# Two-layer conditioned transformer block: layer 1's modulation loads and products moved to later slots, with the first MLP's weights of layer 0 moved four slots later

## The chip, the cores and the metric

The kernel runs on one core of one Trainium2 chip. The metric is the device time of one execution in microseconds. Five engines work in parallel, each through its own instruction list in order: PE (matrix products), DVE (vector), ACT (scalar functions; it also issues some DMAs), POOL and SP (which here only issues DMAs). They wait for each other and for DMAs through semaphores.

## The reference

The input is x, 32 samples of 256 tokens by 288 channels, and one condition vector of 288 channels a sample. Two layers follow each other, and both have this form:

```
mod = silu(cond) @ w_mod + b_mod            # 6 x 288 values a sample: shift, scale, gate for each half
h = layernorm(x) * (1 + scale_a) + shift_a
q, k, v = split(h @ w_qkv + b_qkv)          # 16 heads of 18 channels
q, k = layernorm(q) * g_q, layernorm(k) * g_k   # layer 0 only
x = x + gate_a * (softmax(q k^T / sqrt(18)) v @ w_proj + b_proj)
h = layernorm(x) * (1 + scale_m) + shift_m
x = x + gate_m * (gelu(h @ w1 + b1) @ w2 + b2)  # hidden width 1152
```

All of it is float32. Matrix products are made from operands split in a high and a low part ("hi", "lo"), which are multiplied in three terms.

## The kernel before

The work is a software pipeline over 64 sample passes: passes g = 0 to 31 are layer 0, passes 32 to 63 are layer 1. Time is divided into slots T, from -66 on, and a new pass begins every 16 slots (`SPAN = 16`). Each engine has one function (`slots_pe`, `slots_act`, `slots_dve`, `slots_pool`, `slots_sp`) that runs over all slots and, in each, issues what is due. A slot is not a time: it only sets the order of an engine's list, and semaphore waits do the rest. An engine that waits for nothing runs ahead of the others. The numbers by which things are due are constants at the head of the file, and pass g is due at slot 16g plus the constant. A bank of the matrix unit's output memory is given to each use by `bank_table`, which walks over the same slots.

Around the change these steps matter:

- **Stacks.** The scores of pass g need q and k spread over partitions in a "stack". SP copies them there with 18 DMAs: six small ones of 32 KB (`place_tails`, L1303) and twelve of 128 KB (L1352). For pass 1 they are due at slots -1 to 2, for pass 2 at 15 to 18, for pass 3 at 31 to 34. PE's first score product of pass g (L862, waiting for all 18 DMAs) is due at slot 16g - 12: slot 4 for pass 1, 20 for pass 2, 36 for pass 3, 52 for pass 4.
- **Norm of q and k (layer 0).** ACT writes the reciprocal root (L1031) just after that same slot, SP stores it to device memory (L1324, slot 16g - 26) and reads it back spread out (L1327, L1328, slot 16g - 25, which waits until the store has landed). DVE multiplies with it (L1131, slots 16g - 20 to 16g - 17), ACT and POOL split the result (L1024, L1292), and SP stacks it.
- **Modulation of layer 1.** SP loads two biases and six weight blocks of 324 KB (`load_mod`, L434) at the slots of `MOD_LOAD`. PE makes six products (L565, `MOD_AT[4:]`), and DVE adds the bias to each (L575, `MOD_ROW_AT[4:]`); the first of each waits for all eight loads, since they share a semaphore. DVE copies the rest channels (L583, `MOD_REST_AT[1]`), PE turns the rows (`MOD_TR[1]`), and SP stores them (L1380, 252 KB, `MOD_STORE[1]`).
- **Weights of layer 0's MLP.** They lie over the space of the preparation, so `load_w1` on ACT's queue (1584 KB and a bias in 5 DMAs, `W_AT[0]`) waits for the modulation of layer 1 to be turned and stored; `load_w2` (1296 KB, `W2_AT[0]`) is behind it. The split in hi and lo is on ACT (L752 and L753 for w1, L766 for w2) at `W1_SPLIT[0]` and `W2_SPLIT[0]`, and on DVE (L757, L759, L762 for w1, L770 for w2) one slot later. The first MLP product is due at slot 49.
- **Staging of layer 1's attention weights.** SP loads a third of them at slots 6, 14 and 22, ACT and DVE split it at 16/17, 24/25 and 32/33, and SP stores it (1152 KB for the first two) at 20, 28 and 36.

In one slot SP takes its work in this order: copies of o, the placing of the negated maxima (L1318), the store and the read-back of the roots, the stacks, loads of x, the gate, the store of x, and then this code, which the change touches:

```
if T == MOD_LOAD[0]:   # waits for mod_mm 6, mod_rows_ready 1, scores 1, then the two biases
for j, at in enumerate(MOD_LOAD):
    if T == at: load_mod(q, 1, slice(C * j, C * j + C), S["w_mod_loaded", 2])
if T in MOD_STORE: ...
if T == 18: q.wait_ge(S["mod_stored", 0], 16); q.wait_ge(S["mod_stored", 1], 16)
```

Of the kernel before, what the change touches and what calls it, by code (L numbers as in the profile page):

```python
# [11 lines left out]
B, N, C = 32, 256, 288  # L12
# [53 lines left out]
SPAN = 16  # L66
# [23 lines left out]


MOD_OUT_AT, QKV_HI_AT, QKV_LO_AT, PROJ_REST_AT, PROJ_SCALE_AT, PROJ_HI_AT, PROJ_LO_AT = -56, (-57, -50), (-54, -49), -30, -16, -15, -14
MOD_AT, MOD_ROW_AT = (-36, -36, -27, -26, 6, 7, 8, 9, 10, 11), (-28, -28, -26, -25, 6, 7, 8, 9, 10, 11)
MOD_REST_AT, MOD_TR, MOD_STORE, MOD_LOAD = (-25, 11), (-19, 13), (-13, 15), (-11, -9, -7, -3, -1, 1)
W_AT, W1_SPLIT, W2_SPLIT = (20, SPAN * (B - 1) + 51), (32, SPAN * (B - 1) + 58), (36, SPAN * (B - 1) + 64)
W2_AT = (21, SPAN * (B - 1) + 59)
STAGE_AT = [16, 24, 32]
NEW_QK_AT, NEW_V_AT, NEW_PROJ_AT = SPAN * (B - 1) - 24, SPAN * (B - 1) - 20, SPAN * (B - 1) + 32

# [117 lines left out]
def build(nc, a, out):  # L217
    outer = ExitStack()
    with outer:
# [511 lines left out]
        def load_w1(q, l):  # L731
            if l == 0:
                q.wait_ge(S["proj_w_lo"], 2)
                q.wait_ge(S["spots_ready"], 5)
                q.wait_ge(S["mod_turned"], 24)
                q.wait_ge(S["mod_rows_ready"], 2)
                q.wait_ge(S["mod_stored", 0], 16)
                q.wait_ge(S["mod_stored", 1], 16)
            else:
                q.wait_ge(S["fc1"], FC1_USES * B)  # L740
            w, bias, _ = MLP_NAMES[l]
            for dst, src in raw_moves(w1_raw[:, 2:5, :], w, bias, slice(0, MLP)):
                q.dma_start(dst, src).then_inc(S["w1_loaded"], 16)

        def load_w2(q, l):
            if l > 0:
                q.wait_ge(S["fc2"], TT * B)
            q.dma_start(w2_raw[:, 1], a[MLP_NAMES[l][2]].rearrange("(c p) n -> p c n", p=P)).then_inc(S["w2_loaded"], 16)
# [209 lines left out]
        def slots_act(q):  # L958
            for T in SLOTS:
# [102 lines left out]
                for l in range(LAYERS):  # L1062
                    if T == W_AT[l]:
                        load_w1(q, l)
                    if T == W2_AT[l]:
                        load_w2(q, l)
# [231 lines left out]
        def slots_sp(q):  # L1298
# [7 lines left out]
            for T in SLOTS:  # L1306
# [70 lines left out]
                if T in MOD_STORE:  # L1377
                    l = MOD_STORE.index(T)
                    q.wait_ge(S["mod_rows_ready"], l + 1)
                    q.dma_start(mod_d[l], rows[l][:]).then_inc(S["mod_stored", l], 16)  # L1380
                if T == 18:
                    q.wait_ge(S["mod_stored", 0], 16)
                    q.wait_ge(S["mod_stored", 1], 16)
                if T + 10 in STAGE_AT:
# [44 lines left out]
        @block.sync  # L1429
        def _(q):  # L1430
            prep_sp(q)
            slots_sp(q)
# [25 lines left out]
```

## Time and profile before

| | us |
|---|---|
| median of 3 runs | 2560.09 (2556.29 to 2560.41) |
| the profiled execution | 2560.63 |
| its span | 2558.8 |

The span is what the trace covers; the profiled execution lasted 1.8 us longer than it. Busy shares of the span: PE 93%, PE weight loads 78%, DVE 72%, ACT 64%, POOL 28%. In the page's 40 slices of 64 us PE is busy 5, 5, 6 and 8 tenths in the first four and 9 tenths in nearly all others.

### The profile page before, as it was taken

The numbers are of one execution on the slowest core, as the hardware profiler recorded it, in microseconds if no ns is written. First come the engines' busy times: TensorE is split into PE (matmuls) and PEld (weight loads), VectorE is DVE, ScalarE is ACT, GpSimd is POOL, SyncE is SP. The second block draws the span as 40 slices with busy tenths as digits, with TensorE's granted clock in tenths as the row PEclk, the third lists the DMA queues.
The fourth block names the chain that finished last, engine by engine and source line by source line (L and its number), as shares of the span: only waits on it lengthen the run. The fifth ranks groups of instructions, "written<-read, shape, count | busy, mean of one in ns | idle before, by whom it ended". The sixth has DMA issues, their size and how long they took to land.

```text
span 2558.8 us, 56620 instructions
## 1 busy us (share of the span) xinstructions
PE 2368.6 (93%) x21219; PEld 1988.2 (78%) x21219; DVE 1842.1 (72%) x3456; ACT 1626.4 (64%) x3049; POOL 708.4 (28%) x938
## 2 busy tenths in 40 slices
PE   5568999999999999999899899999999999999998
PEld 3346878878888887887787788888888888888878
DVE  6357777777777777777677777777777777777764
ACT  3256666676676666666566666666676666666653
POOL 2012332332332333233222122222222222223212
PEclk8778999999999999999999999999999999999989
DMA  3776757757656666666856755565566655565531
GB/s 99 134 172 107 122 114 117 122 114 122 116 114 117 116 118 116 114 119 113 141 89 114 144 98 101 95 112 106 97 103 102 114 95 101 97 113 102 95 65 42
DMA packets 259208, 280.91 MB, mean 110 GB/s; under 512 B 25930, under 2 KB 243212, under 8 KB 258936
## 3 DMA queue, kind: packets, MB, share of 16 engines
q1 hardware_dynamic: 245840, 250.24, 56.4%
q10 hardware_dynamic: 13096, 27.04, 4.1%
q8 instruction: 170, 2.79, 0.5%
q14 instruction: 102, 0.84, 0.2%
HBM read 101.86 MB, written 26.73 MB: 50 GB/s over the span
## 4 chain that ended last, share of the span: by engine, by line
PE 50%; DVE 14%; DMA 12%; SPq 7%; issue 7%; POOL 5%; ACT 4%; DVEq 0%; POOLq 0%; ACTq 0%
PE psum L783 11%; DMA attn_k_stack<-attn_qk_hi 9%; PE psum L873 7%; SPq L1352 6%; PE psum_exp L783 5%; PE psum_max L783 5%; DVE attn_maxima L1093 5%; PE psum_exp L849 4%; PE psum L933 4%; PE psum L934 4%; PE psum L935 4%; PE psum_max L862 3%; DVE attn_qk_centred L1131 3%; POOL attn_qk_lo L1292 2%; PE psum L790 2%
## 5 line engine op out<-in xcount | busy, mean ns | idle before, releaser
L969 ACT ACTIVATE attn_probs<-psum_exp 128x1024 f32<-128x1024 f32 x512 | 527.0, 1029 | 401.1 <-PE psum_exp L849 388.2
L1093 DVE TENSOR_REDUCE attn_maxima<-psum_max 128x4 f32<-128x1024 f32 x512 | 620.4, 1212 | 90.1 <-PE psum_max L862 86.1
L1266 POOL TENSOR_TENSOR mlp_x<-mlp_x,mlp_gated 128x288 f32<-128x288 f32 x128 | 103.1, 805 | 1051.6 <-DVE mlp_gated L1110 1051.6
L783 PE MATMUL psum<-attn_ln_split,w_qkv_split 128*128 128x256 f32 (+3 forms) x2240 | 337.6, 296 | 10.1 <-DVE attn_ln_split L1200 6.8
L933 PE MATMUL psum<-mlp_w_fc_hi,mlp_hidden_hi 128*128 128x288 f32 x1152 | 341.7, 297 | 2.9 <-DVE mlp_w_fc_lo L770 2.0
L934 PE MATMUL psum<-mlp_w_fc_lo,mlp_hidden_hi 128*128 128x288 f32 x1152 | 341.4, 296 | 0.0
L935 PE MATMUL psum<-mlp_w_fc_hi,mlp_hidden_lo 128*128 128x288 f32 x1152 | 341.0, 296 | 0.0
L783 PEld LDWEIGHTS psum<-attn_ln_split,w_qkv_split 128*128 128x128 f32 (+3 forms) x2240 | 282.7, 182 | 59.1 <-issue 25.5
L862 PE MATMUL psum_max<-attn_k_stack,attn_q_stack 62*128 62x256 f32 x2048 | 218.9, 292 | 91.5 <-DMA attn_k_stack<-attn_qk_hi 62.7
L873 PE MATMUL psum<-attn_probs,attn_v 128*32 128x256 f32 x4096 | 282.7, 395 | 1.1 <-ACT attn_probs L969 1.1
L849 PE MATMUL psum_exp<-attn_q_stack,attn_k_stack 64*128 64x256 f32 x2048 | 260.2, 332 | 24.2 <-DMA attn_q_stack<-attn_neg_max_lo 12.0
L1224 DVE CAST mlp_hidden_hi<-mlp_hidden 128x512 fp32r<-128x512 f32 (+1 forms) x320 | 127.4, 398 | 175.0 <-ACT mlp_hidden L1051 175.0
L862 PEld LDWEIGHTS psum_max<-attn_k_stack,attn_q_stack 62*128 62x128 f32 x2048 | 159.4, 189 | 113.2 <-DMA attn_k_stack<-attn_qk_hi 56.6
L849 PEld LDWEIGHTS psum_exp<-attn_q_stack,attn_k_stack 64*128 64x128 f32 x2048 | 155.1, 186 | 116.7 <-issue 65.0
L1110 DVE TENSOR_TENSOR mlp_gated<-psum,mlp_gate_and_gated_bias 128x288 f32<-128x288 f32 x128 | 58.3, 456 | 247.3 <-PE psum L935 247.1
L783 PE MATMUL psum_exp<-mlp_ln_split,mlp_w_fc_stacked 128*128 128x256 f32 (+1 forms) x1792 | 229.0, 285 | 2.2 <-ACT attn_probs L969 2.2
L783 PE MATMUL psum_max<-mlp_ln_split,mlp_w_fc_stacked 128*128 128x256 f32 (+1 forms) x1792 | 225.4, 283 | 0.0
L783 PEld LDWEIGHTS psum_exp<-mlp_ln_split,mlp_w_fc_stacked 128*128 128x128 f32 (+1 forms) x1792 | 220.1, 192 | 3.7 <-issue 3.7
L933 PEld LDWEIGHTS psum<-mlp_w_fc_hi,mlp_hidden_hi 128*128 128x128 f32 x1152 | 218.5, 190 | 3.7 <-DVE mlp_w_fc_lo L770 2.3
L783 PEld LDWEIGHTS psum_max<-mlp_ln_split,mlp_w_fc_stacked 128*128 128x128 f32 (+1 forms) x1792 | 219.5, 192 | 0.0
L934 PEld LDWEIGHTS psum<-mlp_w_fc_lo,mlp_hidden_hi 128*128 128x128 f32 x1152 | 218.4, 190 | 0.0
L935 PEld LDWEIGHTS psum<-mlp_w_fc_hi,mlp_hidden_lo 128*128 128x128 f32 x1152 | 218.3, 190 | 0.0
(170 smaller groups left out, 4203.8 us busy)
## 6 DMA issues: line engine op xcount, KB each, us to landing
attn_q_stack<-attn_qk_hi SPq DMA_DIRECT2D x256, 128.0 KB
attn_k_stack<-attn_qk_hi SPq DMA_DIRECT2D x256, 128.0 KB
attn_o_and_sums<-attn_o_transposed SPq DMA_DIRECT2D x256, 128.0 KB, 5.0
mlp_gate_and_gated_bias<-modulation ACTq DMA_DIRECT2D x64, 288.0 KB, 4.1
attn_qk_squares<-qk_rstd SPq DMA_DIRECT2D x32, 512.0 KB
attn_q_stack<-attn_qk_lo SPq DMA_DIRECT2D x128, 128.0 KB
attn_k_stack<-attn_qk_lo SPq DMA_DIRECT2D x128, 128.0 KB
attn_x<-in_x_dram SPq DMA_DIRECT2D x32, 288.0 KB, 8.0
```

What stands on the lines that cost most here:

```text
L783: mm = q.matmul(to, lhs, rhs, start=(i == 0), stop=(i == 6))
L849: mm = q.matmul(ps_exp[:, h, t * N:t * N + N], k_st[i][r, p, t * P:t * P + P], q_st[q_place(g)][r, p, :], start=True, stop=True)
L862: mm = q.matmul(ps_max[:, h, t * N:t * N + N], q_st[q_place(g)][r, p, t * P:t * P + P], k_st[i][r, p, :], start=True, stop=True)
L873: mm = q.matmul(bank[32 * i:32 * i + VW, 0:N], v_sb[g % V_RING][:, t, grp * PV_HEADS + i, :, :].rearrange("p r c -> p (r c)"), probs[pair ...
L933: q.matmul(bank[:, 0:C], h_hi[:, c, cols], w2_hi[:, c, :], start=(c == 0), stop=False)
L934: q.matmul(bank[:, 0:C], h_hi[:, c, cols], w2_lo[:, c, :], start=False, stop=False)
L935: mm = q.matmul(bank[:, 0:C], h_lo[:, c, cols], w2_hi[:, c, :], start=False, stop=(c == CHUNKS - 1))
L969: q.activation(probs[r][:], ps_exp[:], ACT.Exp, scale=SCORE_SCALE).then_inc(S["exps"], 1)
L1093: q.tensor_reduce(maxes[g % 2][:, p // QUARTER, :, p % QUARTER, :], ps_max[:].rearrange("p a (t n) -> p a t n", t=TT), AX.X, ALU.max).then ...
L1224: q.tensor_copy(hi, hidden[use % 2][:, 0:n, :]).then_inc(S["h_hi"], 1)
L1266: q.tensor_tensor(xt, xt, gated2[:], ALU.add).then_inc(S["added2"], 1)
L1352: q.dma_start(fp(st[r:r + MAIN_D, :, :]), fp(parts[order[j]][:, c, :])).then_inc(S["stack_loaded", i], 16)
```

## The change

Only constants change, and the slot of one wait:

```diff
-MOD_AT, MOD_ROW_AT = (-36, -36, -27, -26, 6, 7, 8, 9, 10, 11), (-28, -28, -26, -25, 6, 7, 8, 9, 10, 11)
-MOD_REST_AT, MOD_TR, MOD_STORE, MOD_LOAD = (-25, 11), (-19, 13), (-13, 15), (-11, -9, -7, -3, -1, 1)
-W_AT, W1_SPLIT, W2_SPLIT = (20, SPAN * (B - 1) + 51), (32, SPAN * (B - 1) + 58), (36, SPAN * (B - 1) + 64)
-W2_AT = (21, SPAN * (B - 1) + 59)
+MOD_AT, MOD_ROW_AT = (-36, -36, -27, -26, 10, 11, 12, 13, 14, 15), (-28, -28, -26, -25, 10, 11, 12, 13, 14, 15)
+MOD_REST_AT, MOD_TR, MOD_STORE, MOD_LOAD = (-25, 15), (-19, 17), (-13, 19), (3, 4, 5, 6, 7, 8)
+MOD_DONE = 22
+W_AT, W1_SPLIT, W2_SPLIT = (24, SPAN * (B - 1) + 51), (36, SPAN * (B - 1) + 58), (40, SPAN * (B - 1) + 64)
+W2_AT = (26, SPAN * (B - 1) + 59)
...
-                if T == 18:
+                if T == MOD_DONE:
                     q.wait_ge(S["mod_stored", 0], 16)
                     q.wait_ge(S["mod_stored", 1], 16)
```

The loads of layer 1's modulation go from slots -11 to 1 to slots 3 to 8, its products from 6 to 11 to 10 to 15, its turn from 13 to 17 and its store from 15 to 19. The load of w1 goes from slot 20 to 24 and that of w2 from 21 to 26; the splits go from 32 and 36 to 36 and 40 (ACT), with DVE's part one slot behind. The entries for layer 1 (the second of each pair) are as before.

## Rows read from the trace of the kernel before

**Rows 1.** The page, part 1: busy time of each engine over the span.
```profile
PE 2368.6 (93%) x21219; PEld 1988.2 (78%) x21219; DVE 1842.1 (72%) x3456; ACT 1626.4 (64%) x3049; POOL 708.4 (28%) x938
```

**Rows 2.** Busy time by window: length, engines, PEclk, DMA share, GB/s.
```profile
75.30:111.90 36.60, 18.12 (x117) 13.98 (x117) 16.09 (x27) 11.83 (x28) 4.65 (x7) 0.69 0.77 141
111.90:162.60 50.70, 31.73 (x249) 18.96 (x249) 22.13 (x45) 19.76 (x42) 5.08 (x7) 0.80 0.64 133
162.60:205.70 43.10, 28.91 (x216) 20.03 (x217) 32.59 (x57) 28.60 (x56) 7.92 (x11) 0.78 0.81 183
205.70:247.70 42.00, 37.41 (x313) 29.21 (x313) 30.98 (x53) 25.58 (x52) 9.70 (x13) 0.87 0.60 109
247.70:285.60 37.90, 36.46 (x338) 30.76 (x338) 28.71 (x53) 26.19 (x53) 12.29 (x17) 1.00 0.68 115
```

**Rows 3.** PE's waits from 60 to 252 us: total, times, longest.
```profile
PE psum_max L862 <- DMA attn_k_stack<-attn_qk_hi: 45.2, 5, 17.4
```

**Rows 4.** The chain of waits from 60 to 300 us: start, length, what.
```profile
79.02 3.69 DMA qk_rstd<-attn_qk_rstd
...
83.35 5.56 DMA attn_qk_squares<-qk_rstd
...
103.39 8.48 DMA attn_k_stack<-attn_qk_hi
...
149.10 13.47 DMA attn_k_stack<-attn_qk_hi
...
168.01 7.39 DMA qk_rstd<-attn_qk_rstd
...
197.78 7.87 DMA attn_k_stack<-attn_qk_hi
```

**Rows 5.** Busy time by window, two stretches of 4 us.
```profile
84.00:88.00 4.00, 0.71 (x5) 0.39 (x5) 2.04 (x4) 0.00 (x0) 0.00 (x0) 0.82 0.84 205
...
112.00:116.00 4.00, 4.00 (x36) 1.98 (x37) 1.77 (x3) 0.38 (x1) 0.00 (x0) 0.50 0.00 1
```

**Rows 6.** SP's instructions in order of time: start, length, what.
```profile
94.80 0.44 SPq L434 DMA_DIRECT2D prep_w_mod<-in_L_cond_W_ada_dram  x1
...
121.43 0.55 SPq L1327 DMA_DIRECT2D attn_qk_squares<-qk_rstd  x1
...
140.84 0.44 SPq L1380 DMA_DIRECT2D modulation<-prep_mod_rows  x1
141.33 1.29 SPq L1352 DMA_DIRECT2D attn_q_stack<-attn_qk_hi  x2
```

**Rows 7.** ACT's queue, first DMA of w1.
```profile
144.63 0.42 ACTq L743 DMA_DIRECT2D mlp_w_fc_raw<-in_L_cond_w_dram  x1
```

**Rows 8.** DMA issues from 83.9 to 85.2 us: KB each, us to landing.
```profile
prep_w_mod<-in_L_cond_W_ada_dram SPq DMA_DIRECT2D x2, 324.0 KB, 6.5
```

**Rows 9.** PE's instructions in order of time, 112 to 163 us.
```profile
116.05 2.23 PE L565 MATMUL psum<-prep_w_mod,prep_silu_transposed 96*32 96x288 f32 x6
...
125.96 3.10 PE L565 MATMUL psum<-prep_w_mod,prep_silu_transposed 96*32 96x288 f32 x12
...
162.62 0.80 PE L862 MATMUL psum_max<-attn_k_stack,attn_q_stack 62*128 62x256 f32 x4 [17.38 <-DMA attn_k_stack<-attn_qk_hi]
```

**Rows 10.** DVE's instructions in order of time, 131 to 211 us.
```profile
131.81 0.72 DVE L583 COPY prep_mod_rows_rest<-prep_mod_rows 32x96 f32<-32x96 f32 x4
...
195.38 2.57 DVE L757 TENSOR_TENSOR mlp_w_fc_stacked<-mlp_w_fc_raw,mlp_w_fc_stacked 128x2304 fp32r<-128x2304 f32 x1
197.85 1.43 DVE L759 SCALAR_TENSOR_TENSOR mlp_w_fc_stacked<-mlp_ln_split,s_one_on_low_weight_rows,mlp_w_fc_raw 98x1152 fp32r<-98x1152 f32 x1
...
207.68 2.85 DVE L770 TENSOR_TENSOR mlp_w_fc_lo<-mlp_w_fc_raw,mlp_w_fc_hi 128x2592 fp32r<-128x2592 f32 x1
```

**Rows 11.** Busy time by window, the stretch behind slot 36.
```profile
206.50:222.70 16.20, 12.22 (x106) 7.81 (x108) 15.68 (x25) 9.03 (x19) 2.66 (x4) 0.82 0.45 98
222.70:247.70 25.00, 24.39 (x205) 20.82 (x203) 15.30 (x29) 16.55 (x33) 7.04 (x10) 0.92 0.69 107
```

## The prediction, made before the changed kernel was run

> **What bounds the kernel now.** I began with the busy shares: PE is busy 93% of the span [rows 1], so over the whole it is the bound, and only a stretch in which it stands still can give much. The change touches nothing behind slot 41, and slots run to 1079, so I cut the start into stretches between the first score products of passes 0, 1, 2, 3, 4 and 5 (slots -12, 4, 20, 36, 52, 68) [rows 2]. A pass takes 37.9 us in the last of them, where PE is busy 36.46 us of it. The four before take 36.6, 50.7, 43.1 and 42.0, with PE busy 18.1, 31.7, 28.9 and 37.4. PE's waits name the cause: 45.2 us in five waits for a stack, the longest 17.4 [rows 3]. The chain of waits shows the last DMA of each stack landing 8.48 us after its issue for pass 1, 13.47 for pass 2 and 7.87 for pass 3 [rows 4]. So the start is bound by a loop: root stored, read back, norm, split, 18 stack DMAs, landing, first score product, next root. A gain counts only if a stack lands earlier, a loss counts if it delays the next loop, and whatever is won or lost by slot 52 stays to the end, since nothing behind it waits for a clock. I work out how each of the four first score products moves; + is earlier.
>
> **Slot 4 (111.9 us now).** Three things leave this loop. (a) Two modulation loads are issued right behind the read-back of pass 1's roots, which takes 5.56 us on the chain [rows 4]. Between 84 and 88 us the DMAs move 205 GB/s [rows 5], and at that rate the read-back's 576 KB take 2.9 us, with some 1.2 us before the first data: 4.1 us. I take +1.5, bounds 0 and 2. (b) Two more loads stand among the stack's DMAs [rows 6] (the one shown is issued at 94.80). Each costs SP about 0.5 us of issue, 1.0 together, and 324 KB at 205 GB/s, 1.6 us, 3.2 together. If issue binds the gain is 1.0, if the DMA engines bind it is 3.2; I take +2.0. (c) The loads are now issued behind the stack, three of them before it has landed. If they share the engines with its tail they cost up to 1.5 us; I take -0.5. Sum +3.0, bounds +0.5 and +5.
>
> Here a rule can be weighed. Of the read-back's 5.56 us [rows 4] some 4.4 carry data, which at the rate above is 0.9 MB, and the read-back has 0.59: bytes of later DMAs of the same queue pass before it has landed. The Trainium skill ("DMA: Bandwidth & Descriptors", section on queues, rings and completion order) says that on each DMA engine descriptors of one queue are consumed in ring order. By that rule alone loads behind cost nothing to what is ahead: (a) would be 0, (c) would be 0, and the slot would gain 2.0 in place of 3.0. The trace leans against its plain reading, and the sum goes by the trace.
>
> **Slot 20 (162.6 us now, 50.7 behind slot 4).** Gains first. w1 starts on ACT's queue at 144.63 [rows 7] while pass 2's stack is being issued (from 141.33) [rows 6]. It is the difference that I see between this stack's 13.47 us and the 7.87 and 8.48 of its neighbours: 5.0 to 5.6 us [rows 4]. At slot 24 w1 is issued after PE's slot 20, so it is out of the way: +5.0. The modulation store (0.44 us of issue, ahead of the big copies) goes behind them: +0.5.
>
> Then the new wait. In the loop SP reads the roots back at slot 7, 9.5 us behind PE's slot 4 (121.43) [rows 6]. The blocks of slots 7 and 8 are issued behind the two read-backs, the last at about 9.5 + 1.7 = 11.2 us. Two blocks behind a read-back landed 6.5 us after issue [rows 8]. So the last lands 17.7 us behind slot 4; 14.8 if nothing stands before it (an estimate: 6.5 less the read-back's 2.9), 19.7 if it takes as long as a stack's last DMA, 8.48 [rows 4]. PE gets to its first modulation product (slot 10) earlier than now: that product begins at about 127.5 (the second half of the row of 12), 15.6 behind slot 4, less four products that move back (2.23 and three of some 1.6, 6.9 with their overlap) [rows 9] = 8.7 us. The products and the scores behind them then stand still for 9 us, and slot 10 is 17.7 - 15.6 = 2.1 us later than now. DVE waits with PE for the same loads, and the norm of pass 2 (slots 12 to 15) is queued behind on both. After a standstill the granted clock is 0.50 (the 1.2 GHz level) [rows 5]; I price its return at 1.5 us, bounds 0 and 2.5, by the first product's 2.23 us against 1.6. The copies of slot 11 (0.72 us and a product) [rows 10] leave the front of slot 12's negated maxima: +1.1. Net -2.5, bounds +1 and -5.5. Products in slots 12 to 15 are 6.5 us on PE, beside a stack whose 12 us of issue they mostly hide under; o's last copy at slot 18 may come late: -0.5. Without that cover they would cost up to 3.
>
> Sum for the stretch: +5.0 + 0.5 - 2.5 - 0.5 = +2.5, bounds -3.5 and +6.
>
> **Slot 36 (205.7 us now).** w2 no longer runs beside the store of pass 3's roots, which lands after 7.39 us, against 3.69 for pass 1 [rows 4]: +3.7. But w1 and w2, 2.9 MB, now fall between ACT's slot 24 and the stack, together with a read-back, x and 1.15 MB of stage stores. The DMA share of this stretch is already 0.81 [rows 2]; w1's 1.6 MB more are 8.8 us at the stretch's 183 GB/s and 7.9 at 205, and the share leaves 43.1 x 0.19 = 8.2. So the stack may be issued sooner and land no sooner. ACT's five issues (some 2 us) delay an exponential that PE reaches late anyway. The split of w1 leaves slots 32 and 33, but that shortens only PE's way to a wait for the stack. I take 0, bounds +3 and -5.
>
> **Slot 52 (247.7 us now).** DVE is busy 15.68 of the 16.2 us behind slot 36's scores, and PE 24.39 of the 25 after that [rows 11]: no room on either. In DVE's full stretch now stands w2's low part, 2.85 us. It will hold w1's 2.57 + 1.43 + 0.27 = 4.27 us at slot 37 and w2's 2.85 at slot 41, both ahead of pass 4's norm at slot 44 [rows 10]: 4.3 us more, of which I see nothing that is hidden. ACT's part of w1 falls in PE's wait. I take -4.3, bounds -1.4 (only slot 37's excess counts) and -6.5 (with ACT's 2.4 us of w2 at slot 40).
>
> **Sum.** +3.0 + 2.5 + 0 - 4.3 = +1.2 us. The profiled execution took 2560.63 (span 2558.8 and 1.8 around it), which gives 2559.4. It lies 0.5 above the median of the runs, so against the median I say 2559.
>
> **Rivals.**
> - *The stacks' gain stands, and the rest is hidden (faster).* The last block lands with its 3.6 us or the clock costs nothing (slot 20 gains 5.5 rather than 2.5), the earlier store of the roots gives 2 us at slot 36, and half of DVE's 4.3 us falls into waits for PE. +3 + 5.5 + 2 - 2.2 = +8.3: 2552. For it speaks the 13.47 us, a large and plain stall; against it the full DVE.
> - *The DMA engines in the third stretch (slower).* w1 and w2 pile up before pass 3's stack. If 8.8 us of transfers meet only some 3 us of free share in the part from the load to the stack, the stack lands about 5 us later, and DVE's 4.3 is added in full: +3 + 2.5 - 5 - 4.3 = -3.8, 2564. With the clock's cost at its bound it is 2566. It decides as soon as the stage stores are still in flight when the big copies are issued. Share 0.81 speaks for it; that the stretch held w2 already speaks against it.
> - *It doesn't do what it says:* loads issued behind the stack are served beside it, and pass 1's stack lands as late as now: +0.5 at slot 4, 2561.5.
>
> **How the numbers follow.** Forecast 0.50, hidden rest 0.28, DMA pile 0.15, no earlier stack 0.07. What a measurement of this kernel tells from no change is 0.2%, 5.1 us: below 2555.0 or above 2565.2. The forecast's own spread is some 4 us either way, which leaves 0.08 of all cases at the fast end and 0.05 at the slow one; with most of the first rival (0.22) faster is 0.30, with under half of the second and some of the third slower is 0.14, and the same has 0.56. The range, 2551 to 2566, reaches over both rivals' times.
>
> **What would show it.** Right: PE's wait at slot 4 begins at the same place and ends about 3 us sooner; a new wait of PE for w_mod at slot 10, near 9 us; pass 2's last stack DMA landing within 7 to 9 us; the stretch to slot 36 near 43 us with DMA share above 0.9; the stretch to slot 52 near 46 us with w1's split inside. Wrong: no wait at slot 10, which would leave PE's early start to the norm of pass 2 and give 3 us or more; a stretch of 42 us to slot 52; or a stack 3 that lands after 12 us.

## The result, and the profile after

The changed kernel takes 2571.77 us (median of 5 runs, 2567.29 to 2572.78); the kernel before, timed with it, 2556.29. The ratio is 1.0055, 95% interval 1.0042 to 1.0067. By the medians it is 15.5 us slower (11 to 17 by the interval), where 2559 and no change were forecast, and outside the range of 2551 to 2566. The profiled execution took 2572.48 us, 11.85 more than that of the kernel before.

I cut its start as before, between the first score products of passes 0 to 5. This is the view of busy time by window: length, then PE, PE's weight loads, DVE, ACT, POOL, PEclk, DMA share, GB/s. Lines of the changed kernel are one higher than before (L863 is the score product, L566 the modulation product).

```profile
76.60:110.50 33.90, 17.03 (x117) 13.07 (x117) 16.08 (x27) 11.55 (x28) 4.62 (x7) 0.75 0.57 84
110.50:166.60 56.10, 38.79 (x251) 22.07 (x251) 22.76 (x45) 19.85 (x42) 4.50 (x7) 0.71 0.63 127
166.60:215.00 48.40, 27.07 (x217) 19.11 (x217) 26.66 (x54) 26.23 (x55) 8.17 (x11) 0.75 0.88 207
215.00:261.70 46.70, 38.52 (x313) 30.15 (x313) 35.26 (x56) 27.73 (x53) 9.66 (x13) 0.83 0.50 93
261.70:299.80 38.10, 36.53 (x340) 30.82 (x340) 28.71 (x53) 26.16 (x53) 12.28 (x17) 1.00 0.68 114
```

Against [rows 2] the four stretches changed by -2.7, +5.4, +5.3 and +4.7 us, together +12.7; the fifth is as it was (38.1 against 37.9). Another 1.3 us of the trace's difference lies ahead of slot -12, where the change has moved nothing; that slot comes between 74.4 and 76.6 us in the twelve traces of this case. The forecast had -3.0, -2.5, 0 and +4.3. So the first and the last came out as numbers, and the two in the middle did not.

PE's waits in the changed kernel, from 75 to 262 us (total, times, longest), hold one that was not there:

```profile
PE psum_max L863 <- DMA attn_k_stack<-attn_qk_hi: 39.2, 5, 13.8
PE psum_max L863 <- DVE attn_maxima L1094: 10.7, 4, 6.0
PE psum L942 <- DVE attn_maxima L1094: 10.3, 4, 4.2
PE psum L566 <- DMA prep_w_mod<-in_L_cond_W_ada_dram: 9.4, 1, 9.4
```

PE's instructions in order of time show that wait and what follows it. Each row of x6 is one product:

```profile
129.19 3.06 PE L566 MATMUL psum<-prep_w_mod,prep_silu_transposed 96*32 96x288 f32 x6 [9.39 <-DMA prep_w_mod<-in_L_cond_W_ada_dram]
...
133.33 3.08 PE L566 MATMUL psum<-prep_w_mod,prep_silu_transposed 96*32 96x288 f32 x6
...
136.66 3.09 PE L566 MATMUL psum<-prep_w_mod,prep_silu_transposed 96*32 96x288 f32 x6
...
147.19 1.64 PE L566 MATMUL psum<-prep_w_mod,prep_silu_transposed 96*32 96x288 f32 x6
```

The standstill of 9.4 us is the one forecast. The products then take 3.1 us and not 1.6: the granted clock of the stretch behind it is 0.50, the 1.2 GHz level, although PE is busy all the time (the clock comes back at 142.5, 13.3 us after the first product began):

```profile
129.20:142.00 12.80, 12.80 (x47) 5.16 (x51) 4.49 (x8) 2.25 (x3) 0.00 (x0) 0.50 0.01 2
```

In the third stretch the chain of waits goes through x for the residual, which SP asks for behind the read-back and POOL needs first, 16.28 us after its issue; the roots' store lands in 4.03, where it took 7.39 [rows 4]:

```profile
171.49 4.03 DMA qk_rstd<-attn_qk_rstd
175.53 0.57 SPq L1328
...
176.15 0.57 SPq L1329
...
176.77 16.28 DMA mlp_x<-in_x_dram
193.05 0.07 issue
193.12 0.93 POOL mlp_x L1263
```

DVE's longest wait there is for the read-back, which lands 15.2 us after its second issue (176.15 to 191.37):

```profile
DVE attn_qk_centred L1132 <- DMA attn_qk_squares<-qk_rstd: 9.3, 1, 9.3
```

w2, issued at 175.70 on ACT's queue, ran beside it and took 22.8 us. From 175.5 to 177.3 us the packets of ACT's queue (q10) take 68% of the 16 DMA engines' time and those of SP's (q1) 29%:

```profile
mlp_w_fc_raw<-in_L_cond_w_dram ACTq DMA_DIRECT2D x1, 1296.0 KB, 22.8
...
q10 hardware_dynamic: 80, 0.37, 68.1%
q1 hardware_dynamic: 66, 0.13, 29.2%
```

In the fourth stretch the chain holds the splits of both weights on DVE, where before it held w2's alone [rows 10]:

```profile
217.04 2.46 DVE mlp_w_fc_stacked L758
219.50 1.33 DVE mlp_w_fc_stacked L760
...
231.13 2.85 DVE mlp_w_fc_lo L771
```

### The profile page after: what moved, and what is told of

Its sections match the earlier page's. It is cut to its first block, busy times and chain, and to the rows that moved or that the text cites. A ratio compares the mean times of both kernels' runs of the same rounds, so it can differ in the third digit from the quotient of the medians.

```text
span 2570.7 us, 56620 instructions
## 1 busy us (share of the span) xinstructions
PE 2372.7 (92%) x21219; PEld 1990.3 (77%) x21219; DVE 1839.4 (72%) x3456; ACT 1624.5 (63%) x3049; POOL 705.4 (27%) x938
## 4 chain that ended last, share of the span: by engine, by line
PE 51%; DVE 14%; DMA 12%; SPq 8%; issue 7%; POOL 5%; ACT 4%; DVEq 0%; POOLq 0%; ACTq 0%
PE psum L784 12%; DMA attn_k_stack<-attn_qk_hi 9%; PE psum L874 7%; SPq L1353 6%; PE psum_exp L784 5%; PE psum_max L784 5%; DVE attn_maxima L1094 5%; PE psum_exp L850 4%; PE psum L934 4%; PE psum L935 4%; PE psum L936 4%; PE psum_max L863 3%; DVE attn_qk_centred L1132 2%; PE psum L791 1%; POOL attn_qk_lo L1293 1%
## 5 line engine op out<-in xcount | busy, mean ns | idle before, releaser
L1094 DVE TENSOR_REDUCE attn_maxima<-psum_max 128x4 f32<-128x1024 f32 x512 | 620.6, 1212 | 85.2 <-PE psum_max L863 81.3
L863 PE MATMUL psum_max<-attn_k_stack,attn_q_stack 62*128 62x256 f32 x2048 | 219.3, 293 | 84.8 <-DMA attn_k_stack<-attn_qk_hi 55.9
L863 PEld LDWEIGHTS psum_max<-attn_k_stack,attn_q_stack 62*128 62x128 f32 x2048 | 160.4, 190 | 105.5 <-DMA attn_k_stack<-attn_qk_hi 48.3
```

Source lines behind the costliest of these rows:

```text
L863: mm = q.matmul(ps_max[:, h, t * N:t * N + N], q_st[q_place(g)][r, p, t * P:t * P + P], k_st[i][r, p, :], start=True, stop=True)
L1094: q.tensor_reduce(maxes[g % 2][:, p // QUARTER, :, p % QUARTER, :], ps_max[:].rearrange("p a (t n) -> p a t n", t=TT), AX.X, ALU.max).then ...
```

## The experiments

Ten kernels, all timed against the kernel before. The table gives each one's four stretches (us between first score products, from the start times of PE's rows) and the ratio with its interval. In the first, third and fourth stretch, kernels that share the order of work agree within 0.4 to 1.3 us. The second is less sure: four kernels do the same up to slot 20 (changed, modulation only, splits back, weights later) and take 56.1, 56.5, 56.9 and 53.3 us. Each kernel has one trace. The total times do not follow the stretches closely: "weights later" is 7.7 us above the kernel before by its stretches and 14.2 by the medians, "dense after the wait" 13.9 and 23.9. The trace of the kernel before is itself one of its slower executions (2560.63 us, where the medians of its runs beside the other kernels are 2555.1 to 2559.3).

| kernel | to slot 4 | to 20 | to 36 | to 52 | sum | ratio (95%) |
|---|---|---|---|---|---|---|
| before | 36.6 | 50.7 | 43.1 | 42.0 | 172.3 | 1 |
| changed | 33.9 | 56.1 | 48.4 | 46.7 | 185.1 | 1.0055 (1.0042 to 1.0067) |
| weights only | 36.6 | 45.8 | 49.1 | 46.1 | 177.6 | 1.0022 (1.0011 to 1.0032) |
| modulation only | 33.5 | 56.5 | 45.4 | 41.6 | 177.0 | 1.0023 (1.0012 to 1.0033) |
| splits back | 33.6 | 56.9 | 48.1 | 41.8 | 180.3 | 1.0037 (1.0023 to 1.0051) |
| weights later | 33.5 | 53.3 | 47.2 | 46.0 | 180.0 | 1.0058 (1.0042 to 1.0075) |
| loads early | 33.6 | 41.9 | 48.4 | 46.6 | 170.4 | 1.0002 (0.9992 to 1.0011) |
| warm | 33.6 | 49.5 | 49.4 | 46.4 | 178.8 | 1.0027 (1.0014 to 1.0040) |
| dense after the wait | 33.6 | 57.7 | 48.9 | 46.1 | 186.2 | 1.0082 (1.0063 to 1.0101) |
| early, old weight slots | 33.7 | 44.1 | 46.0 | 41.5 | 165.3 | 0.9965 (0.9952 to 0.9977) |
| early, w2 at 37 | 33.7 | 43.2 | 41.7 | 46.8 | 165.5 | 0.9975 (0.9961 to 0.9989) |
| early, w2 at 42 | 33.6 | 43.9 | 41.4 | 43.4 | 162.2 | 0.9966 (0.9953 to 0.9979) |

**Weights only.** The kernel before with the weights' line of the change:

```diff
-W_AT, W1_SPLIT, W2_SPLIT = (20, ...), (32, ...), (36, ...)    # W2_AT 21
+W_AT, W1_SPLIT, W2_SPLIT = (24, ...), (36, ...), (40, ...)    # W2_AT 26
```

> The kernel before with only the MLP weights of layer 0 moved (w1 loaded at slot 24, w2 at 26, splits at 36 and 40), the modulation as before. Stretches between first score products: 36.6, 50.7, 43.1, 42.0 us before and 33.9, 56.1, 48.4, 46.7 after. My theory: the weights own one gain and two losses. Stretch to slot 4 stays 36.6; stretch to slot 20 falls to 45 to 46, since w1 no longer runs beside pass 2's stack; stretch to slot 36 is 47 to 49, since w1 and w2 now run beside pass 3's read-back (DVE's wait for attn_qk_squares near 9 us, 2 to 4 before); stretch to slot 52 is 46 to 47. Total 3 to 5 us slower than before. Rival: the two late losses come down from the standstill at slot 10 (low clock, late work), and then stretches three and four stay at 43 and 42 here, and the kernel is 5 us faster than before.

As my theory had it in all four stretches: -4.9 us in the second, +6.0 in the third (49.1, at the upper end) and +4.1 in the fourth, in a kernel that never stands still at slot 10. In its third stretch DVE waits 7.9 us for the read-back and x takes 15.58, as in the changed kernel. The rival is out: the two late losses belong to the weights. In time it is 5.6 us slower than before, a little more than the 3 to 5 expected.

**Splits back.** `W1_SPLIT[0]` 36 to 32 and `W2_SPLIT[0]` 40 to 36 in the changed kernel.

> The changed kernel with only the splits of the MLP weights back at slots 32 and 36. My theory: DVE's full stretch behind slot 36 holds 4.3 us less, so the stretch to slot 52 falls from 46.7 to 42 to 43 us and the others stay (33.9, 56.1, 48.4; w2's landing, 22.8 us after issue, is by then past). Some 4 us faster than the changed kernel, 8 to 10 slower than before. Rival: the fourth stretch is long because of the late stack or the low clock, and stays at 46 to 47.

The fourth stretch fell to 41.8 and nothing else moved by more than 0.8. DVE's busy time in it is again what it was before, 30.98 us [rows 2], against 35.26 in the changed kernel:

```profile
214.80:256.60 41.80, 37.28 (x311) 29.18 (x311) 30.98 (x53) 25.57 (x52) 9.75 (x13) 0.88 0.57 104
```

**Weights later.** `W_AT[0]` 24 to 28 and `W2_AT[0]` 26 to 32 in the changed kernel.

> The changed kernel with w1 loaded at slot 28 and w2 at 32 (24 and 26), splits unchanged. My theory: pass 3's read-back then has the DMA engines to itself: DVE's wait for it falls from 9.3 us to under 3, and the stretch to slot 36 from 48.4 to 42 to 45 us (the loads may now lie beside the stack, which costs up to 3). Other stretches as in the changed kernel, unless w1's later landing holds ACT at slot 36. 4 to 6 us faster than the changed kernel. Rival: the read-back is late for the stage stores, not for w1 and w2, and the third stretch stays at 48.

Half right. DVE's wait for the read-back in this stretch fell to 0.3 us, so w1 and w2 were what held it, but the stretch fell only to 47.2, and in time the kernel is no faster than the changed one (1.0058 against 1.0055). The same transfers, issued at 173.9 and 190.3, now stood in the way of the negated maxima and of pass 3's stack, as the chain of this kernel shows (a last stack DMA takes 6.8 to 8.7 us in stretches where no MLP weights run beside it):

```profile
179.00 12.00 DMA attn_q_stack<-attn_neg_max_lo
...
196.52 13.53 DMA attn_k_stack<-attn_qk_hi
```

The second stretch is 2.8 us shorter than the changed kernel's, although no part of the edit lies ahead of slot 20. PE does the same work in the same order there and stands still for 9.8 us. What differs is the clock: it comes back 6.5 us after the first product began (at 128.89), within the second product, and the third is already at full speed:

```profile
133.03 2.81 PE L566 MATMUL psum<-prep_w_mod,prep_silu_transposed 96*32 96x288 f32 x6
...
135.97 1.64 PE L566 MATMUL psum<-prep_w_mod,prep_silu_transposed 96*32 96x288 f32 x6
```

In the changed kernel, "splits back" and "modulation only" the same work had to go on for 13.3, 14.1 and 13.3 us first. Why it took half as long here no run shows.

**Loads early.** The six blocks are issued before SP waits for the roots of pass 2:

```diff
-MOD_LOAD = (3, 4, 5, 6, 7, 8)
+MOD_LOAD = (3, 3, 4, 4, 5, 5)
```

> The changed kernel with the six modulation blocks loaded at slots 3, 3, 4, 4, 5, 5 in place of 3 to 8, so that SP issues all of them ahead of its wait for pass 2's roots. My theory: the last block lands by 118 us, PE does not stand still at slot 10 (9.4 us in the changed kernel), the clock stays up, and the stretch to slot 20 falls from 56.1 to 43 to 47 us; the roots' store may land 2 us later. 9 to 12 us faster than the changed kernel. Rival 1: the wait moves to the negated maxima at slot 8, which are then behind 2 MB of loads, and the gain is under 4. Rival 2: the products themselves at slots 10 to 15, not the wait, hold pass 2's norm, and the stretch stays above 51.

The second stretch fell by 14.2 us to 41.9, the shortest of all. PE's wait for the blocks is gone, and the clock is 0.91 over the stretch. Of the first rival there is a sign, a wait of PE of 2.6 us for the negated maxima, but not its cost:

```profile
109.40:151.30 41.90, 32.41 (x251) 19.92 (x251) 23.05 (x45) 19.98 (x42) 4.63 (x7) 0.91 0.83 171
```

The three later kernels with the same slots for the modulation took 44.1, 43.2 and 43.9: they wait 1.8 to 2.8 us at the same place, and at or just behind that wait the clock falls to 0.50 once more for some 3.5 us, which it doesn't do here. Against "weights only" (45.8), where the six products stand at slots 6 to 11, these four are 1.7 to 3.9 us better. So moving loads and products together was a gain (which of the two gives it, no run separates), and what spoilt it was how late the data were asked for.

**Modulation only.** The changed kernel with the weights' slots of before.

> The changed kernel with the MLP weights' slots as before (w1 20, w2 21, splits 32 and 36): the modulation's part of the change alone. ACT's slot 20 now waits for the modulation's store of slot 19, so w1 leaves about when pass 2's stack has landed. My theory: stretches 33.6, 56 to 58 (standstill and low clock as in the changed kernel), 43 to 46 (w1 and w2 lie ahead of pass 3's read-back), 42. Some 4 us slower than before, 8 faster than the changed kernel. Rival: w1 and w2 cost the third stretch as much wherever they stand, 48.

As expected, 45.4 in the third stretch and 41.6 in the fourth. Against the kernel before, w1 and w2 cost 2.3 us more in the third stretch when they start right behind pass 2's stack (w1 at 166.6), and 6.0 more when they start at slots 24 and 26.

**Warm.** The changed kernel with work in place of the standstill:

```diff
+if n == 4:      # the first of layer 1's products, slot 10
+    for i in range(40):
+        q.matmul(bank[:, 0:P], ident[:], ident[:], start=True, stop=True)
 mod_product(q, 2 + n, bank)
```

> The changed kernel, with 40 idle products (identity by identity, 128 columns, float32, some 0.2 us each at 2.4 GHz, 8 to 9 us together) put in PE's list at slot 10 ahead of the product that waits for the modulation's loads; they write a bank that this product overwrites. PE no longer stands still, it works through the wait. My theory: the standstill lets the granted clock fall to 0.50 and the six products then take 3.1 in place of 1.6 us; kept at work, the clock stays at 1.0 and the stretch to slot 20 falls by 5 to 8 us from 56.1, though the wait for the loads is the same. Rival: the clock comes down from the products themselves, or has no part, and the stretch stays above 54.

The added block took 9.09 us, PE then waited only 0.4 for the loads, and the stretch fell by 6.5 us. The products behind it take 1.6 us:

```profile
117.95 9.09 PE L839 MATMUL psum<-identity 128*128 128x128 f32 x80
127.47 1.64 PE L567 MATMUL psum<-prep_w_mod,prep_silu_transposed 96*32 96x288 f32 x6 [0.42 <-DMA prep_w_mod<-in_L_cond_W_ada_dram]
```

The first modulation product still begins 18.6 us behind slot 4, as in the changed kernel (18.7), so the wait is the same and the 6.5 us are the clock's. Against "weights later" (53.3), where the clock came back sooner, it is 3.8, and against "splits back" (56.9) 7.4.

**Dense after the wait.** 20 such products ahead of the second modulation product.

> The changed kernel with 20 identity products (128 by 128 weights, 0.23 us each at 2.4 GHz, twice that at 1.2) ahead of the second modulation product: added work of 5 to 9 us behind the standstill, none in it. It asks why the clock, which in the kernel before is back at 1.0 some 6 us after a standstill, takes 13 us in the changed one. Theory: the modulation products (96 by 32 weights) do not raise it and dense ones do; the clock is back within the added block and the products behind it take 1.6 in place of 3.1 us, which pays back 4 to 6 of the added 5 to 9 us. The stretch to slot 20 is 56 to 60. Rival: the low clock lasts 13 us whatever PE does, all products still take 3.1 us until then, and the stretch is 62 to 65.

The clock came back within the added block, and the next modulation products are at full speed:

```profile
128.04 3.06 PE L567 MATMUL psum<-prep_w_mod,prep_silu_transposed 96*32 96x288 f32 x6 [9.77 <-DMA prep_w_mod<-in_L_cond_W_ada_dram]
...
132.19 5.81 PE L839 MATMUL psum<-identity 128*128 128x128 f32 x40
137.93 1.64 PE L567 MATMUL psum<-prep_w_mod,prep_silu_transposed 96*32 96x288 f32 x6
```

5.8 us of added work lengthened the stretch by 1.6 against the changed kernel. The rival, 13 us whatever PE does, is out. But the theory isn't shown either: the clock came back 6.4 us after the first product began, and in "weights later" it came back after 6.5 with the modulation products alone. With one trace of each, this run can't tell the kind of work from that spread.

**Early loads with the old weight slots.**

> The modulation moved as in the change but its six blocks loaded at slots 3, 3, 4, 4, 5, 5, and the MLP weights' slots as before. My theory: 33.6, 42, 43 to 46, 42 us: 6 to 10 us faster than before. Rival: w1, which now starts when pass 2's stack has landed, delays the roots' store and read-back of pass 3 as in the changed kernel, the third stretch is 48, and the gain over before is 3 to 4.

165.3 us of stretches against 172.3 and a ratio of 0.9965, 8.4 us by the medians: the first version faster than before. The second stretch (44.1) is 2 us above what I expected, for the clock as told under "loads early". The third (46.0) is at the upper end of it: the roots' store takes 9.83 us there, beside w1 and w2.

**w2 at slot 37**, split at 45 and 46.

> As the one with early loads and the old weight slots, but w2 is loaded at slot 37 and split at 45 (ACT) and 46 (DVE). Its 1296 KB then lie behind pass 3's stack, where the DMA share is near 0, and its 2.85 us on DVE leave the full stretch behind slot 36. My theory: 33.6, 42, 42 to 44, 39 to 41 us: 3 to 5 us faster than the kernel with the old weight slots, 10 to 13 faster than before. Rival: the loop's next read-back (pass 4) meets w2, and the fourth stretch is 42 or more.

The third stretch came out (41.7, where w2 no longer runs), the fourth went the rival's way: 46.8. So the kernel is no faster than the one with the old weight slots (2550.5 and 2550.9 us). w2 was issued at 198.03, just ahead of the roots' store at 198.47, whose read-back could only be issued at 205.80, and its split stood in ACT's list ahead of the exponential of slot 45.

**w2 at slot 42**, split at 47 and 48, `MOD_DONE` 21 (ahead of the load of the gate in slot 22, which reads what it waits for).

> As the kernel with early loads, w1 at slot 20 and its split at 32, but w2 is loaded at slot 42, behind pass 4's read-back (slot 39) and not, as at slot 37, ahead of the roots' store, and split at 47 (ACT) and 48 (DVE), where DVE waits for the MLP. The wait for the modulation's store is at slot 21. Stretches of the kernel with w2 at slot 37: 33.7, 43.2, 41.7, 46.8 us. My theory: the first three stay and the fourth falls to 40 to 43, since the chain of the 46.8 held the roots' store at 7.3 us and ACT's split in the norm of pass 4. 12 to 16 us faster than before (0.9940 to 0.9955), 3 to 6 faster than the best so far. Rival: w2 collides with x and the negated maxima of slots 42 to 45 instead, and the fourth stretch stays at 46.

43.4 us in the fourth stretch and 162.2 in all, the least of any version. In time it is 2545.9 us in the median of 10 runs against 2555.1 for the kernel before; the ratio of 0.9966 is 8.7 us, less than the 12 to 16 expected, and within its interval the same as the version with the old weight slots. x for pass 1's residual, issued at 203.81 just before w2 at 203.86, takes 10.81 us in its chain (7.00 for pass 0), so w2 still collides with it.

## Why the prediction was wrong

**Slot 4, forecast +3.0: right as a number, in part by luck.** The gain is 2.7 us, and 2.9 to 3.1 in the other kernels with the modulation moved. Its terms came out otherwise. (a), the two loads behind the read-back, was to give 1.5: with nothing behind it the read-back takes 5.25 us here (4.8 to 5.0 in the others) against 5.56 [rows 4], so 0.3 to 0.8. (b), the two loads among the stack's DMAs, was to give 2.0: from the read-back's landing to the issue of the last stack DMA it is 1.4 us less. (c) was to cost 0.5: the last stack DMA took 7.95 us against 8.48, so loads issued behind the stack did not hold it. The store of the roots gives the last 0.35. By ring order alone (a) and (c) would have been 0 and the sum 2.0, and its terms are no further off than mine.

**Slot 20, forecast +2.5, measured -5.4: this is the step that failed most, by a term that was mis-sized.** The gain of w1's move was right (5.0 forecast, 4.9 in "weights only"). The wait was nearly right too: first product 17.7 us behind slot 4 forecast, 18.7 measured, a standstill of 9 forecast and 9.4 measured. What failed is "I price its return at 1.5 us, bounds 0 and 2.5, by the first product's 2.23 us against 1.6". "Warm" puts the term at 6.5 us in this kernel. The price was already too low for the kernel before: the product of 2.23 us [rows 9] is only the last work at the low clock there, and PE had then worked at 0.50 since slot 4, with score products of 0.80 us that later take 0.40. Its clock comes back 5.4, 5.9 and 3.7 us after the first score products at 111.9, 162.6 and 205.7, and at half speed each of these costs half its length, up to 3 us. The first modulation product of the changed kernel stands at the head of such a stretch and not at its end. That the stretch was then 13.3 us long was in no row of the kernel before, and why it was is open: with the same work it was 13.3, 14.1, 13.3 and 6.5 us in four kernels. Without the clock, "warm" still stands 3.7 us above "weights only", where my other terms made 1.0; 1.0 of the difference is the later landing of the blocks, and the rest, 1.7, I can't assign.

**Slot 36, forecast 0, bounds +3 and -5, measured -5.3: wrong, by a term put at nothing.** The rival of the DMA pile named the right cause and the right size, 5 us, and the wrong place. I looked for it at the stack. It came at the read-back (15.2 us) and at x (16.3, before 6.7), which ran beside w1 and w2 on the other queue. I had put w1's issue behind slot 24's work on ACT; in the trace ACT's queue hands it over at 173.0, ahead of the splitting of the stage (173.8 to 175.9) that stands before it in ACT's list and ahead of the read-back at 175.5, and w2 at 175.7. So the earlier store of the roots, +3.7 forecast and 3.4 measured, bought nothing. The last stack DMA took 7.2 us, as ever. "Weights only" has the same loss without a standstill at slot 10, and "w2 at slot 37" loses nothing here.

**Slot 52, forecast -4.3: right.** 4.7 us, and 4.9 back with the splits. DVE was full there [rows 11], and the split had no cover.

**The chances.** 7.9 of the 13.9 us by which the four stretches missed the forecast (+1.2) come from the second and 5.3 from the third. 0.14 for slower was too low, since both hung on work that I moved into stretches whose DMA share and clock I had seen to be tight. Both losses lie outside their bounds, the third stretch's just (-5.3 for -5), the second's clearly (-5.4 for -3.5): the bound of the clock, 2.5 us, was taken from one product and not from the whole stretch at the low clock that the same rows show.

## What to carry to other kernels

Price a load's new place from both ends: what it leaves, and when the instruction that needs it is reached. Here the products' data came 9 us late, because the loads stood behind a wait of SP's that they didn't need; issuing them ahead of it took 14 us out of the stretch, the standstill and the low clock behind it. A transfer moved out of one critical DMA's way lands in the way of another when the chain is a loop of DMAs: look for a hole before the next link, in the queues' issue times and not in slots. And a standstill of PE costs the wait and the clock: price the clock by the whole stretch at the low level that the rows show behind other standstills, not by one product, and allow for more, since here the same code had 6.5 and 14.1 us of it.

## What was not expected of the hardware

- After a standstill of 9.4 to 9.8 us with the same work behind it, the granted clock stayed at 0.50 (1.2 GHz) for 13.3, 14.1, 13.3 and 6.5 us in four kernels (changed, splits back, modulation only, weights later), although PE's busy time was nearly all of it (12.80 of 12.8 us from 129.2 on in the changed kernel). With 40 products of identity by identity in the place of the standstill it stayed at 1.00 for the 9.1 us of these and the 14.6 us behind them.
- w1 and w2 (1584 and 1296 KB) on ACT's queue made a read-back of 576 KB on SP's take 15.2 us (pass 1's, without them, 5.6 [rows 4]) and a load of x of 288 KB 16.3 (6.7). The Trainium skill ("DMA: Bandwidth & Descriptors", section "Issuing engines are not separate DMA queues") says that DMAs of different issuers run on the same engines and interleave, and this trace agrees, as far as its rows go: from 175.5 to 177.3 us ACT's queue had 68% of the 16 engines' time and SP's 29%, and the critical transfers on the other queue were not spared.
